# Scan stage of a two-layer macaron network: the input product moves to PSUM, the decay to a ring in SBUF, and small row work moves from VectorE to TensorE and ScalarE

## The reference, cut to what matters

```python
xz = einsum('bld,ed->bel', hidden, W_in);  x, z = split(xz)           # 256 channels each
xc = gate[0]*silu(conv(x, w1, dil=1)+b1) + gate[1]*silu(conv(x, w2, dil=2)+b2)
dt_low, B, C = split(xc^T @ W_x)                                      # 64, 16, 16
delta = softplus(dt_low @ W_dt + b_dt);  A = -exp(A_log)              # A: 256 x 16
for t:  h = h*exp(delta_t*A) + delta_t*B_t*x_t;   y_t = sum_n h[n]*C_t[n]
y = (y + D*xc) * silu(z);   out = y @ W_out
```

## Time and profile before

| | |
|---|---|
| median of three runs | 3625.48 us |
| the profiled execution's own time | 3626.36 us |
| its span | 3624.6 us |
| busy, of the span | PE 69%, DVE 67%, POOL 47%, ACT 38% |
| scan stage | from about 1782 to about 3270 us of the span |

### The profile page before, as it was taken

How to read it: one execution, slowest core, us unless ns; L and a number is a source line. 1 busy time by engine, 2 the same in 40 slices (tenths; PEclk the granted TensorE clock), 3 DMA queues, 4 the chain that set the end, 5 groups by cost and what they waited for, 6 DMA issues and landing times. The chain is left out here.

```text
span 3624.6 us, 49800 instructions
## 1 busy us (share of the span) xinstructions
PE 2508.1 (69%) x12480; PEld 1742.2 (48%) x12480; DVE 2423.3 (67%) x6334; ACT 1387.8 (38%) x2576; POOL 1716.5 (47%) x1350
## 2 busy tenths in 40 slices
PE   2329976666499922499667777777777777757992
PEld 2319974444399922399522333323232323326992
DVE  3604446677544477255469999999999999984553
ACT  0015543323155500255344444444444444424551
POOL 2745541232345547455324555555555555563551
PEclk9999997767599955699888888888888888878996
DMA  7137861110177732477423333333333333316776
GB/s 250 53 102 226 227 176 36 36 47 29 47 230 226 203 107 64 140 226 228 141 99 108 113 113 106 106 115 106 105 105 105 105 105 103 108 60 191 228 227 178
DMA packets 262504, 478.86 MB, mean 132 GB/s; under 512 B 37309, under 2 KB 173467, under 8 KB 262272
## 3 DMA queue, kind: packets, MB, share of 16 engines
q1 hardware_dynamic: 202576, 388.64, 36.1%
q0 software_dynamic: 34816, 68.00, 5.3%
q10 hardware_dynamic: 25008, 21.11, 1.8%
HBM read 383.22 MB, written 98.54 MB: 133 GB/s over the span
## 5 line engine op out<-in xcount | busy, mean ns | idle before, releaser
L1267 POOL TENSOR_TENSOR ssm_HC<-ssm_H,ssm_BC 128x1024 f32<-128x1024 f32 x256 | 600.0, 2344 | 675.9 <-DVE ssm_dBx L1333 607.4
L1107 PE MATMUL ssm_psY<-ssm_HC,ident 128*128 128x512 f32 x1024 | 641.0, 760 | 336.4 <-POOL ssm_HC L1267 334.7
L1339 DVE TENSOR_TENSOR_SCAN ssm_H<-ssm_psD,ssm_dBx 128x1024 f32<-128x1024 f32 x256 | 586.4, 2290 | 40.0 <-ACT ssm_psD L1208 23.3
L1107 PEld LDWEIGHTS ssm_psY<-ssm_HC,ident 128*128 128x128 f32 x1024 | 219.0, 232 | 685.7 <-POOL ssm_HC L1267 469.0
L1208 ACT ACTIVATE ssm_psD<-ssm_delta,ssm_A 128x511 f32<-128x511 f32 x256 | 176.0, 687 | 688.7 <-DVE ssm_H L1339 688.7
L1333 DVE TENSOR_TENSOR ssm_dBx<-ssm_ux,ssm_BC 128x1024 f32<-128x1024 f32 x256 | 323.4, 1263 | 8.2 <-issue 5.6
L336 POOL DMA_INDIRECT xslots<-att_r_xn,att_r_idx x128 | 126.3, 987 | 322.7 <-DVE att_r_idx L316 220.2
L1072 PE MATMUL ssm_psA<-ssm_hT,ssm_Wtap 128*128 128x512 f32 x512 | 241.6, 606 | 4.3 <-ACT ssm_hT L1159 4.3
L656 POOL DMA_INDIRECT c_back<-c_yr,c_to_row x144 | 139.8, 971 | 155.7 <-DVE c_yr L731 133.7
L656 POOL DMA_INDIRECT a_back<-a_yr,a_to_row x144 | 139.8, 971 | 155.5 <-DVE a_yr L731 133.6
L656 POOL DMA_INDIRECT d_back<-d_yr,d_to_row x144 | 139.8, 971 | 155.3 <-DVE d_yr L731 133.3
(11 more groups left out here) (506 smaller groups left out, 5559.5 us busy)
## 6 DMA issues: line engine op xcount, KB each, us to landing
ssm_BC<-bc_rows SPq DMA_DIRECT2D x128, 1024.0 KB
a_W<-in_l_pack SPq DMA_DIRECT2D x72, 514.0 KB
b_W<-in_l_pack SPq DMA_DIRECT2D x72, 514.0 KB
c_W<-in_l_pack SPq DMA_DIRECT2D x72, 514.0 KB
d_W<-in_l_pack SPq DMA_DIRECT2D x72, 514.0 KB
a_xs<-xslots SPq DMA_DIRECT2D x72, 131.0 KB
b_xs<-xslots SPq DMA_DIRECT2D x72, 131.0 KB
c_xs<-xslots SPq DMA_DIRECT2D x72, 131.0 KB
```

Source lines behind the costliest of these rows:

```text
L1107: last = nc.tensor.matmul(psY[:, dt, :], k.ident[:, :], HC[:, n % RP, (dt + n) % DT, :], start=(n == 0), stop=(n == NB - 1))
L1267: nc.gpsimd.tensor_tensor(HC[:, n % RP, :, :], H[:, n % RH, :, :], BC[:, n // CHUNK % SLOTS, 1, n % CHUNK:n % CHUNK + 1, :].to_broadcast([ ...
L1339: nc.vector.tensor_tensor_scan(flat(H[:, n % RH, :, :]), flat(psD[:, odd:odd + DT, :]), flat(dBx[:, n % RB, :, :]), 0.0, ALU.mult, ALU.add ...
```

## The change

What it does, in the order of the diff:

- The gathered rows of s+2 are added to each other on TensorE into `psR` (identity, `Take.pe`, at n=4), and VectorE adds that sum to X once (`dve_sum`). `stats(s+2)` moves from n=7 to n=6, the root of that norm on ScalarE from n=9 to n=7, `normalize(s+2)` from n=10 to n=9.
- Norm rows, for the block's own norm and for the router: VectorE makes only a scale and a shift per row, ScalarE applies them (`act_apply`, `act_0`), and ScalarE also rescales the four rows of X. The router's `normed` thus comes from ScalarE at n=6, `pe_1a` goes to n=7, `pe_1b` to n=9, `act_1` to n=8, `dve_2a` to n=10.
- The router's eight semaphores per set of scatters become one.
- `delta*u*B` goes to PSUM (`psX`, three rows) in two instructions of 512 columns; the second waits for the scan before it. The decays go to a ring of four in SBUF (`dA`), and their wait is for the scan three further back. `ux` loses its third row.
- `D*xc` enters `psY` as two matmuls with a diagonal matrix ahead of state 0's, and `gated` is one multiplication out of PSUM.
- `mix`: the first product is done on ScalarE at the end of `silu` (`halved`), and VectorE's part moves from n=9 to n=10. `step_sizes_1`: the addition of 1 is done on ScalarE, between its Exp and its Ln.

```diff
+    def dve_0(self, nc, dve, chain, s, b, turn):
+        n.dve_finish(nc, dve, chain, s)
+        n.dve_scales(nc)
+        chain(nc.vector.scalar_tensor_tensor(out=n.odd[:, :], in0=n.mean[:, :], scalar=-0.5, in1=n.rstd[:, 0, :], op0=ALU.mult, op1=ALU.mult))
+        nc.vector.tensor_scalar(n.rstd[:, 0, :], n.rstd[:, 0, :], 0.5, 1.0, ALU.mult, ALU.add).then_inc(n.scaled, 1)
+        self.free(dve, b, turn)
+        nc.vector.tensor_scalar(self.xn[:, b, :, D], k.token[:, self.four(s)], 1.0, None, ALU.mult)
+    def act_0(self, nc, act, s, b, turn):
+        self.free(act, b, turn)
+        n.act_apply(nc, act, self.xn[:, b, :, :], s).then_inc(self.normed, 1)
+        for j in range(self.tiles):
+            nc.scalar.activation(x, x, ACT.Identity, bias=n.odd[:, j:j + 1], scale=n.rstd[:, 0, j:j + 1])
...
+    def pe(self, nc, pe, s, b, turn, out):                       # Take
+        pe.wait_ge(self.arrived[b], turn * 16 + 16)
+        for c in range(TOPK):
+            last = nc.tensor.matmul(out, self.k.ident[:, :], self.rows[:, b, :, c * D:(c + 1) * D], start=(c == 0), stop=(c == TOPK - 1))
+    def dve_sum(self, nc, dve, s, total):
+        dve.wait_ge(self.summed, s + 1)
+        nc.vector.tensor_tensor(x, x, total, ALU.add).then_inc(self.taken, 1)
...
-            def total(s, n):
+            def total(s, b, n):
                 pe.wait_ge(hc_ready, s * NB + n + 1)
+                if n == 0:
+                    if positive(s):
+                        pe.wait_ge(y_ready, s)
+                    for dt in range(DT):
+                        nc.tensor.matmul(psY[:, dt, :], diag[:, dt, :], xc[:, b, dt, :], start=True, stop=False)
...
                 nc.scalar.activation(zs[:, b, :, :], zs[:, b, :, :], ACT.Silu).then_inc(z_done, 1)
                 act.preload_act_table_set("natural_log_exp_and_others")
+                act.wait_ge(silu_done, s + 1)
+                nc.scalar.activation(xc[:, b, :, :], pre[:, 0:DT, :], ACT.Identity, scale=gates[:, 0:1]).then_inc(halved, 1)
...
             def decay(s, b, n):
-                if positive(t - 1):
-                    act.wait_ge(h_ready, t - 1)
-                nc.scalar.activation(psD[:, 2 * odd, 1:], delta[:, b, 0, 1:], ACT.Exp, scale=A[:, 0, n:n + 1])
-                if positive(t):
-                    act.wait_ge(h_ready, t)
-                nc.scalar.activation(psD[:, 1, 1:], delta[:, b, 1, 1:], ACT.Exp, scale=A[:, 1, n:n + 1]).then_inc(dA_ready, 1)
+                if positive(s * NB + n - RA + 1):
+                    act.wait_ge(h_ready, s * NB + n - RA + 1)
+                for dt in range(DT):
+                    last = nc.scalar.activation(dA[:, n % RA, (dt + n) % DT, 1:], delta[:, b, dt, 1:], ACT.Exp, scale=A[:, dt, n:n + 1])
+                last.then_inc(dA_ready, 1)
...
             def gated(s, b):
                 dve.wait_ge(y_summed, s * NB + NB)
-                for dt in range(DT):
-                    last = nc.vector.scalar_tensor_tensor(out=v[:, dt, :], in0=xc[:, b, dt, :], scalar=col[:, dt, 3:4], in1=psY[:, dt, :], op0=ALU.mult, op1=ALU.add)
-                nc.vector.tensor_tensor(v[:, :, :], v[:, :, :], zs[:, b, :, :], ALU.mult).then_inc(y_ready, 1)
+                nc.vector.tensor_tensor(v[:, :, :], psY[:, :, :], zs[:, b, :, :], ALU.mult).then_inc(y_ready, 1)
...
-                nc.vector.tensor_tensor(dBx[:, n % RB, :, :], ux[:, b, odd:odd + DT, :], BC[:, c % SLOTS, 0, n % CHUNK:n % CHUNK + 1, :].to_broadcast([P, DT, SEQ]), ALU.mult).then_inc(dBx_done, 1)
+                nc.vector.tensor_tensor(psX[:, 2 * odd, :], ux[:, b, 0, :], BC[:, c % SLOTS, 0, n % CHUNK, :], ALU.mult)
+                if positive(s * NB + n):
+                    dve.wait_ge(h_ready, s * NB + n)
+                nc.vector.tensor_tensor(psX[:, 1, :], ux[:, b, 1, :], BC[:, c % SLOTS, 0, n % CHUNK, :], ALU.mult).then_inc(dBx_done, 1)
...
-                nc.vector.tensor_tensor_scan(flat(H[:, n % RH, :, :]), flat(psD[:, odd:odd + DT, :]), flat(dBx[:, n % RB, :, :]), 0.0, ALU.mult, ALU.add).then_inc(h_ready, 1)
+                nc.vector.tensor_tensor_scan(flat(H[:, n % RH, :, :]), flat(dA[:, n % RA, :, :]), flat(psX[:, odd:odd + DT, :]), 0.0, ALU.mult, ALU.add).then_inc(h_ready, 1)
```

More of the change, by code:

```diff
@@ L136, in __init__ @@
         self.stats = st.sb(f"{name}_stats", [P, tiles, 6])
-        self.mean, self.odd, self.var = (st.sb(f"{name}_{n}", [P, tiles]) for n in ("mean", "odd", "var"))
+        self.scaled = st.sem(f"{name}_scaled")
+        self.mean, self.odd, self.var, self.shift = (st.sb(f"{name}_{n}", [P, tiles]) for n in ("mean", "odd", "var", "shift"))
         self.shifted, self.root, self.newton, self.rstd = (st.sb(f"{name}_{n}", [P, self.w, tiles]) for n in ("shifted", "root", "newton", "rstd"))
@@ L170, in dve_finish, with dve_scales, act_apply @@
         chain(nc.vector.scalar_tensor_tensor(out=self.rstd[:, :, :], in0=self.newton[:, :, :], scalar=1.5, in1=self.root[:, :, :], op0=ALU.add, op1=ALU.mult))
+    def dve_scales(self, nc):
+        return nc.vector.scalar_tensor_tensor(out=self.shift[:, :], in0=self.mean[:, :], scalar=-1.0, in1=self.rstd[:, self.w - 1, :], op0=ALU.mult, op1=ALU.mult)
+    def act_apply(self, nc, act, out, s):
+        act.wait_ge(self.scaled, s + 1)
+        for j in range(self.tiles):
+            last = nc.scalar.activation(out[:, j, 0:D], rows_of(self.k.X, s * self.tiles + j), ACT.Identity, bias=self.shift[:, j:j + 1], scale=self.rstd[:, self.w - 1, j:j + 1])
+        return last
     def dve_apply(self, nc, out, s):
@@ L208, in four, with free @@
         return bass.ds(s * self.tiles, self.tiles)
+    def free(self, eng, b, turn):
+        if not self.whole and not (isinstance(turn, int) and turn == 0):
+            eng.wait_ge(self.scattered[b], turn * (self.copies * 16))
+    def dve_0(self, nc, dve, chain, s, b, turn):
+        k, n = self.k, self.norm
+        n.dve_finish(nc, dve, chain, s)
[5 more added lines that the diff above has]
+    def act_0(self, nc, act, s, b, turn):
+        n = self.norm
+        self.free(act, b, turn)
+        n.act_apply(nc, act, self.xn[:, b, :, :], s).then_inc(self.normed, 1)
+        for j in range(self.tiles):
+            x = rows_of(self.k.X, s * self.tiles + j)
+            nc.scalar.activation(x, x, ACT.Identity, bias=n.odd[:, j:j + 1], scale=n.rstd[:, 0, j:j + 1])
     def dve_1(self, nc, dve, chain, s, b, turn):
@@ L213, in dve_1 @@
         n.dve_finish(nc, dve, chain, s)
-        if not self.whole and not (isinstance(turn, int) and turn == 0):
-            for i in range(self.copies):
-                dve.wait_ge(self.scattered[self.copies * b + i], turn * 16)
+        self.free(dve, b, turn)
         nc.vector.tensor_scalar(self.xn[:, b, :, D], k.token[:, self.four(s)], 1.0, None, ALU.mult)
@@ L400, in sp_pads @@
         else:
-            for s in range(2 * self.copies):
-                sp.wait_ge(self.scattered[s], TILES // self.tiles // 2 * 16)
+            for b in range(2):
+                sp.wait_ge(self.scattered[b], TILES // self.tiles // 2 * self.copies * 16)
         for e in range(EXPERTS):
@@ L1228, in between @@
                         to_hT(s + 1)
+                    if n == 7 and there(s, 2):
+                        N.act_root(nc, act, s + 2)
                     if n == 8:
@@ L1297, in step_sizes_1 @@
             def step_sizes_1(s, b):
[L1299 to L1300 removed]
+                dve.wait_ge(one_ready, s + 1)
                 chain(nc.vector.scalar_tensor_tensor(out=rest[:, :, :], in0=rest[:, :, :], scalar=-1.0, in1=soft, op0=ALU.add, op1=ALU.subtract))
@@ L1401, in _ @@
             R.norm.dve_stats(nc, chain, s)
-            R.dve_1(nc, dve, chain, s, b, s // 2)
+            R.dve_0(nc, dve, chain, s, b, s // 2)
             R.dve_2a(nc, dve, chain, s, b)
```

113 lines of the change are left out of this document (65 added, 48 removed).

## The result

The changed kernel takes 3518.64 us (median of four, 3517.86 to 3519.25) against 3625.47 us (3625.4 to 3643.66): a ratio of 0.9693 with an interval of 0.9663 to 0.9723. The profiled execution took 3519.25 us, its span is 3517.4 us. That is 107 us less, where 114 were forecast.

The account below looks back on a forecast made before the run. DVE's list was taken to bound the scan stage, busy 1279 of 1385 us. Savings of 172.4 us less 17, 15, 22 and 4 gave 114 us: 3512 from the profiled 3626.4, 3511 against the median; range 3465 to 3580.

Parts of the forecast that it names:

- gated: End of a state sequence: two multiply-adds leave DVE, the multiplication stays; 1.44 us saved x16 = 23.0.
- dve_1: Router's norm rows and X rows on DVE: one wait and four small operations stay; 2.45 us saved x15 = 36.8.
- Gathered rows: Two additions and a wait on DVE become one addition out of PSUM; 1.73 us saved x12, sum 22.5.
- the lost cover: HC of state 7 runs late into a bare product, one or two per sequence; 15 us lost, range 0 to 30.
- own norm rows: Block's own norm: four DVE instructions become one small one; 0.85 us saved x14 = 12.
- today's waits: DVE's waits for ACT's work or at the scan behind it, before the change; 46.4 us counted as saved.
- The halves: Product in two instructions into PSUM: 0.06 to 0.07 us more each, x256 = 17; bounds 0 and 43.
- The remaining waits for ACT: DVE still waiting for decays of states 10 and 15: 1.5 us per sequence, x15 = 22; bounds 0 and 46.
- PE as the pace (1): Steps 1 to 7, partly at 1.2 GHz: silu and state 10's scan 4 us later, 60 us lost, 3571; chance 0.13.
- All as wished (2): Scan stage: no waits left, products at the price of one, no late HC; 168 us saved, 3458; chance 0.07.
- A dear PSUM destination (3): DVE's half products: writing PSUM costs 0.53 us more each, 273 in place of 17, 3768; chance 0.06.
- Rival 4: POOL's indirect DMA slips between the halves and delays the second: 112 us lost, no change, 3624; chance 0.06.

Follow-up runs that it names:

- e10: e3 with D*xc back on VectorE and no diagonal matmuls; 3629.21 us, ratio 0.9669 to the kernel before on its chip.
- e9: The same kernel as e3, run on another chip; 3612.97 us, ratio 0.9628 to the kernel before on that chip.
- e8: The changed kernel with D*xc back on VectorE and no diagonal matmuls; 3630.33 us, ratio 0.9707 to the kernel before on its chip.
- e3: The changed kernel with ScalarE's decay of state 10 made at n=8, ahead of silu; 3490.83 us, ratio 0.9622 to the kernel before.
- e11: e3 with the product as one instruction of 1024 columns instead of two halves; 3631.63 us, ratio 0.9682 to the kernel before on its chip.
- e7: The changed kernel with mix's first product back on VectorE; 3633.29 us, ratio 0.9704 to the kernel before on its chip.
- e12: The changed kernel with the product whole and in SBUF, decay ring of two places; 4006.31 us, ratio 1.0676 to the kernel before on its chip.

## Why the prediction was right

**The sum, step by step.** Per sequence, from the table of steps, with 0.07 us for each step's two halves taken out:

- `gated`: 1.44 forecast, 1.33 + 0.07 = 1.40 in the step of state 1, and 21.8 of 23.0 us in e10. Right, but see below.
- `dve_1`: 2.45 forecast, 2.99 + 0.07 = 3.06 at state 5. The surplus is L169: its 1006 ns were counted as staying, and 446 are left, since HC is not late there.
- Gathered rows with the lost cover: 1.73 less 15/12 = 0.48 forecast, 1.61 + 0.14 = 1.75 at states 6 and 7, less 0.25 at state 8. So the additions gave what was forecast (1.75 against 1.73), and the cover cost about 0.3 us a sequence, some 4 us, not 15. That is the step that failed most: late products above 1 us, one or two per sequence by the forecast, are two in the whole stage.
- States 9 and 10 (own norm rows 0.85, `mix` 0.79, today's waits 1.1 + 0.4, less the 1.5 that remains): 1.64 forecast, 1.26 + 0.14 = 1.40 measured.
- States 14 and 15 (`step_sizes_1` 0.72, third row 0.60, the scan of state 15 1.55): 2.87 forecast, 2.17 + 0.47 + 0.14 = 2.78 measured.
- The halves: 0.07 forecast, 3.59 against 3.51 in the bare step. The prologue: +4 forecast, +4.5 measured. But the time to the first scan is 79.7 us in e9 and 79.4 in e8, which has no diagonal matmuls, so this agreement shows nothing about PE.
- The remaining waits for ACT: 22 us forecast for states 10 and 15. At state 10 it was 28.5, and moving one decay gave 24.4 of the stage back. The forecast let the convolutions end when scan 8 starts; they end 1.05 us later, since PE works without a gap, and ACT's copy of z out of PSUM (1.07 us) wasn't on the path that it added up.
- The ends: in the middle a sequence is 8.8 us shorter, but the first only by 0.3 (it finishes no other), and the last two by 6.1 and 4.4. The forecast took most terms 15 times.

So the number owes something to luck. `dve_1` and the cover gave some 9 and 12 us more than forecast, the ends and state 10 less, and the 13 us of attention brought 120 back to 107. The mechanism held: DVE's list is the pace, and the time came off with what left it.

**The rivals.** PE as the pace (1): not of the stage, where PE still waits 198 us for POOL, but of the way to silu. There its condition came true at the full clock: no gap on PE in the steps of states 1 to 7, and the scan of state 10 late by 1.6 us a sequence instead of the 4 that this rival put on the lower clock. The forecast had that loss in the term for ACT. All as wished (2): it lacked the state-10 wait; e3, which removes it, has a scan stage 144.5 us shorter than before, against this rival's 168. A dear PSUM destination (3): no, 690 ns against 685. Beside it stands the rule weighed in the prediction: the Trainium skill's table ("VectorE: DVE Perf Modes", the section on the TRN2 errata) would have put up to 62 cycles on each half, if a destination in PSUM paid what its source does. No such charge shows here, neither for a PSUM source (662 ns, L480) nor for a destination. Rival 4 had the mechanism and not the sign: POOL's indirect DMA does slip in at the halves (it starts in the middle of the first), but it is what lets HC start 0.6 us earlier, and not a stall of the second half. Its price was forecast as a loss of up to 112 us; e11 measures a gain of 19 us from the halves, against one product whose bare step is as long. This gain, never in the sum, and the cover that was not needed are one thing: HC is no longer late.

**What the sum hid.** It added terms as if each came back one for one. In the kernel after they don't. e8 puts work back on DVE ahead of scan 10 and the stage is no longer, since DVE otherwise waits there for ACT; e7 puts it back behind that scan and takes as much of the wait away on ACT's side. `mix` (11.9), D*xc (23.0) and part of the norm rows were thus worth nothing to anyone who would take them back singly. The total was right all the same, because the wait had been subtracted once, for the whole. With the wait gone (e10) a term is worth its full time.

**Not foreseen:** attention's 13 us. They go with the granted clock; no edit was shown to cause them.

## What to carry to other kernels

When DVE's list is the pace, sum up what leaves it, but then look for the next in-order list (here PE's convolutions, then ACT's silu and decay), state by state and not by its share of the whole stage, where PE was busy for 77% and yet had no gap on the way to silu. Test each edit again with that wait removed: an edit that looks worthless may be worth its full time. Where a ring has free places, ask for the next item before the long work, not behind it. And cutting a long instruction in two at a small cost can pay through what slips between the halves on another engine.

## What the runs showed of the hardware

- A POOL instruction that reads SBUF and a DVE instruction with two SBUF inputs exclude one another for nearly their whole time: a scan with two such inputs (e12) makes HC 4064 ns and a bare step 5.55 us, and with one input in PSUM HC takes 2350 beside it. The Trainium skill says so too ("SBUF — State Buffer", SBUF: two separate sides): an exclusive lock, held by the one that starts first. The trace agrees, in these numbers.
- The indirect DMA's own work on POOL takes part in this: 1144 ns on average with half products, 1440 with whole ones.
- The attention stage of one and the same program took 437.9 us on one chip (e3, granted clock 0.69) and 463.4 on another (e9, 0.66), with 267 and 317 us of it at the granted 1.2 GHz.
- Five executions of one program on one chip (e3) took 3472.03 us at a mean granted clock of 0.857, and 3490.81 to 3492.91 at 0.852 or 0.853.
